# A routed expert loop: gate and up with the weights held, deeper rings, and longer lags between its stages

## The reference, cut to what matters

```python
tidx, tw = _gate(x, gate_w, gate_bias)          # 8 experts of 64, weights scaled by 2.5
w_dense = jnp.zeros((T, E), tw.dtype).at[jnp.arange(T)[:, None], tidx].add(tw)
def body(acc, ws):
    wg, wu, wdn, cw = ws                        # 256x128, 256x128, 128x256
    hmid = jax.nn.silu(x @ wg) * (x @ wu)
    return (acc + cw[:, None] * (hmid @ wdn), None)
y, _ = jax.lax.scan(body, jnp.zeros_like(x), (We_gate, We_up, We_down, w_dense.T))
```

## Time and profile before

| | us |
|---|---|
| median of 3 runs (lowest, highest) | 973.32 (966.68, 979.72) |
| the profiled execution | 971.8 |
| its span, first to last instruction | 970.0 |
| expert loop, first index copy to last scatter | 654 to 938 |

### The profile page before, as it was taken

How to read it: one execution, slowest core, us unless ns; L and a number is a source line. 1 busy time by engine, 2 the same in 40 slices (tenths; PEclk the granted TensorE clock), 3 DMA queues, 4 the chain that set the end, 5 groups by cost and what they waited for, 6 DMA issues and landing times. The chain is left out here.

```text
span 970.0 us, 19279 instructions
## 1 busy us (share of the span) xinstructions
PE 754.2 (78%) x6571; PEld 492.9 (51%) x6571; DVE 468.9 (48%) x1284; ACT 259.9 (27%) x519; POOL 269.6 (28%) x304
## 2 busy tenths in 40 slices
PE   5799998775769989989978897546768666747646
PEld 4355556454535554664457776324556445533215
DVE  4423335776745323235638868886523322322216
ACT  1121214744502121212644302231112211211150
POOL 1020002013412000000315611406556655654420
PEclk9899999998869999979985568877778877887778
DMA  9999991101887999812972101007666656658858
GB/s 342 386 354 397 412 405 57 37 2 36 317 318 271 341 411 390 348 34 48 212 172 67 39 4 43 1 1 254 199 180 214 207 183 195 210 170 254 254 182 317
DMA packets 70781, 200.40 MB, mean 207 GB/s; under 512 B 11912, under 2 KB 37744, under 8 KB 64944
## 3 DMA queue, kind: packets, MB, share of 16 engines
q1 hardware_dynamic: 60720, 176.29, 52.3%
q0 software_dynamic: 7680, 20.98, 7.0%
q10 hardware_dynamic: 2304, 2.10, 0.7%
HBM read 185.51 MB, written 13.83 MB: 206 GB/s over the span
## 5 line engine op out<-in xcount | busy, mean ns | idle before, releaser
L2000 PE MATMUL ps<-moe_wset,moe_xgT 128*128 128x256 f32 (+1 forms) x320 | 109.7, 477 | 58.4 <-issue 25.5
L2120 POOL DMA_INDIRECT moe_xg<-xn_rows,moe_idx x80 | 78.5, 981 | 111.1 <-DVE moe_idx L2069 85.8
L2000 PEld LDWEIGHTS ps<-moe_wset,moe_xgT 128*128 128x128 f32 (+1 forms) x320 | 64.9, 226 | 76.0 <-issue 56.0
L2129 POOL DMA_INDIRECT y_rows<-moe_ysb,moe_row x80 | 79.1, 989 | 42.9 <-issue 29.0
L2082 DVE TENSOR_TENSOR moe_hrow<-moe_hs,ps 128x128 f32<-128x128 f32 x80 | 22.9, 287 | 107.0 <-ACT moe_hs L2104 74.2
L2104 ACT ACTIVATE moe_hs<-ps 128x128 f32<-128x128 f32 x80 | 22.3, 278 | 163.4 <-PE ps L2000 98.4
L1469 POOL TENSOR_TENSOR ss_dec<-ss_dec,ss_cT 128x256 f32<-128x256 f32 x48 | 39.7, 862 | 91.0 <-ACT ss_dec L1424 51.1
L2077 DVE COPY moe_xgT<-ps 128x256 f32<-128x256 f32 x80 | 33.9, 424 | 62.3 <-remote 36.8
L2015 PE MATMUL ps<-moe_wset,moe_hT 128*128 128x256 f32 (+1 forms) x160 | 59.9, 463 | 3.2 <-issue 2.1
L1282 PE MATMUL ps<-xnT,w_win 128*128 128x512 f32 x128 | 58.4, 614 | 0.0
L299 PE MATMUL ps<-x0ctxT,x0qcur 128*64 128x512 f32 (+1 forms) x256 | 48.5, 534 | 7.5 <-issue 5.4
(11 more groups left out here) (404 smaller groups left out, 1424.2 us busy)
## 6 DMA issues: line engine op xcount, KB each, us to landing
x0ctxT<-ctx_T SPq DMA_DIRECT2D x8, 3202.0 KB, 18.2
x1ctxT<-ctx_T SPq DMA_DIRECT2D x8, 3202.0 KB, 13.0
x0ctxN<-ctx SPq DMA_DIRECT2D x8, 3072.0 KB
x1ctxN<-ctx SPq DMA_DIRECT2D x8, 3072.0 KB
moe_wset<-moe_gate_up SPq DMA_DIRECT2D x80, 256.0 KB
moe_wset<-L_ffn_We_down SPq DMA_DIRECT2D x80, 128.0 KB
moe_yg<-y_rows SPq DMA_DIRECT2D x7, 1024.0 KB, 10.9
ss_dec<-seg_rows SPq DMA_DIRECT2D x8, 768.0 KB, 17.0
```

What stands on the lines that cost most here:

```text
L2000: mm = pe.matmul(ps[c * n_:(c + 1) * n_, 2 + a2, 0:2 * FE], xgT[:, a2, h, c * n_:(c + 1) * n_], src[:, aw, h, :], start=h == 0, stop=h == ...
L2120: nc.gpsimd.indirect_dma_start(out=xg[:, a4, :], out_offset=None, in_=xn_rows, in_offset=bass.IndirectOffsetOnAxis(ap=idx[:, a4:a4 + 1], a ...
L2129: nc.gpsimd.indirect_dma_start(out=y_rows, out_offset=bass.IndirectOffsetOnAxis(ap=row[:, a4:a4 + 1], axis=0), in_=ysb[:, a4, :], in_offse ...
```

## The change

Gate and up: the weights become the stationary operand and the turned token rows move, so the product comes out turned (hidden units on partitions, tokens in columns), gate in PSUM columns 0 to 127 and up in 128 to 255 of the same bank. The turning of the hidden rows (`turn_hidden`), its copy `hT`, and two semaphores go. In a halves tile both experts write all 128 partitions, in different columns. `xg`, `ysb`, `idx`, `row` become rings of eight, `xgT` and silu of four, the hidden product of eight; PSUM has four banks for gate and up instead of two.

The lags: TensorE's step n holds transposes(n), gate_up(n-2), down(n-6). VectorE's holds idx(n), the xgT copy(n-7), the product(n-10), row(n-12). ScalarE's holds silu(n), ysb(n-4). GpSimd's holds gather(n), scatter(n-14). SP's `load` is untouched; it still waits for down of tile n-8. `diag` gets its memory ahead of the rings instead of after them, and the last block waits for eight scatter semaphores.

```diff
+            diag = own("diag", [P, NT // 2, 8, P])
-            xg = ring("xg", [P, 4, D])
-            xgT = ring("xgT", [P, 2, DH, P])
+            xg = ring("xg", [P, RING, D])
+            xgT = ring("xgT", [P, 4, DH, P])
-            ysb = ring("ysb", [P, 4, D])
-            hrow = ring("hrow", [P, 2, FE])
+            ysb = ring("ysb", [P, RING, D])
+            silu = ring("silu", [P, 4, FE])
+            hidT = ring("hidT", [P, RING, FE])
...
+            GU, DOWN, AHEAD = 2, 6, 7
...
                     def gate_up(n, m, g, late):
-                        wait(pe, s_hh, k - 1)
+                        wait(pe, s_hh, k - 3)
                         n_ = P if late is None else P // 2
-                        for h in range(DH):
+                        for x in range(2):
                             for c, src in enumerate((wset,) if late is None else (wset, wset2)):
-                                mm = pe.matmul(ps[c * n_:(c + 1) * n_, 2 + a2, 0:2 * FE], xgT[:, a2, h, c * n_:(c + 1) * n_],
-                                               src[:, aw, h, :], start=h == 0, stop=h == DH - 1)
+                                for h in range(DH):
+                                    mm = pe.matmul(ps[:, 2 + a4, x * P + c * n_:x * P + (c + 1) * n_], src[:, a8, h, x * FE:(x + 1) * FE],
+                                                   xgT[:, a4, h, c * n_:(c + 1) * n_], start=h == 0, stop=h == DH - 1)
                         mm.then_inc(s_gu, 1)
-                    def turn_hidden(n, m):
...
-                        pe.transpose(ps[:, 6 + a2, 0:P], hrow[:, a2, :], ident[:]).then_inc(s_hx, 1)
                     def down(n, m, g, late):
-                        k, (a4, a2) = n - 3, slots(m, 3)
-                        pe.wait_ge(s_hc, k + 1)
+                        k, a8, b = n - DOWN, (m - DOWN) % RING, (m - DOWN) % 2
+                        pe.wait_ge(s_hh, k + 1)
...
 vector:
-                        if isinstance(n, int) and n == 3:
+                        if isinstance(n, int) and n == AHEAD - 1:
                             for i in range(8):
                                 weight_third(i)
-                        if live(3):
+                        lag = AHEAD
+                        if live(lag):
...
+                        lag = AHEAD + GU + 1
+                        if live(lag):
...
+                            nc.vector.tensor_tensor(hidT[:, a8, :], silu[:, a4, :], ps[:, 2 + a4, P:2 * P], ALU.mult).then_inc(s_hh, 1)
+                        lag = AHEAD + DOWN - 1
...
 gpsimd:
-                        if live(7):
+                        lag = AHEAD + DOWN + 1
+                        if live(lag):
...
 last block, sync:
-                    for m in range(4):
-                        sp.wait_ge(s_ys[m], rounds * (RING // 4 * 16))
+                    for m in range(RING):
+                        sp.wait_ge(s_ys[m], rounds * 16)
```

More of the change, by code:

```diff
@@ L2036, in _ @@
                         transposes(first * RING + m, m, first)
-                        gate_up(first * RING + m, m, first, 0 if m >= 1 else None)
-                        turn_hidden(first * RING + m, m)
-                        down(first * RING + m, m, first, 0 if m >= 3 else None)
+                        gate_up(first * RING + m, m, first, 0 if m >= GU else None)
+                        down(first * RING + m, m, first, 0 if m >= DOWN else None)
                     with pe.Fori(1, second) as late:
@@ L2090, in step @@
                             if not early(k):
-                                dve.wait_ge(s_ys[a4], turn_of(g, m, 6) * 16)
-                            nc.vector.tensor_scalar(row[:, a4:a4 + 1], rowt[:, ds(k, 1)], 0, None, ALU.add).then_inc(s_rw, 1)
-                        if isinstance(n, int) and 4 <= n < 16:
-                            for i in ((n + 4,) if n < 12 else (2 * n - 8, 2 * n - 7)):
+                                dve.wait_ge(s_ys[a8], turn_of(g, m, lag) * 16)
+                            nc.vector.tensor_scalar(row[:, a8:a8 + 1], rowt[:, ds(k, 1)], 0, None, ALU.add).then_inc(s_rw, 1)
@@ L2095, in step @@
+                        if isinstance(n, int) and 7 <= n < 16:
+                            for i in ((n + 1,) if n < 9 else (2 * n - 8, 2 * n - 7)):
                                 weight_third(i)
-                    run(dve, step, 6)
+                    run(dve, step, AHEAD + DOWN - 1)
                 @block.scalar
@@ L2100, in step @@
                         if live(0):
-                            k, (a4, a2) = n, slots(m, 0)
+                            k, a4 = n, m % 4
                             act.wait_ge(s_gu, k + 1)
-                            wait(act, s_hh, k - 1)
-                            nc.scalar.activation(hs[:, a2, :], ps[:, 2 + a2, 0:P], ACT.Silu).then_inc(s_si, 1)
-                        if live(2):
-                            k, (a4, a2) = n - 2, slots(m, 2)
+                            wait(act, s_hh, k - 3)
+                            nc.scalar.activation(silu[:, a4, :], ps[:, 2 + a4, 0:P], ACT.Silu).then_inc(s_si, 1)
+                        lag = DOWN - GU
+                        if live(lag):
+                            k, a8, b = n - lag, (m - lag) % RING, (m - lag) % 2
                             act.wait_ge(s_dn, k + 1)
                             if not early(k):
-                                act.wait_ge(s_ys[a4], turn_of(g, m, 2) * 16)
-                            nc.scalar.copy(ysb[:, a4, :], ps[:, 4 + a2, 0:D]).then_inc(s_yc, 1)
-                    run(act, step, 2)
+                                act.wait_ge(s_ys[a8], turn_of(g, m, lag) * 16)
+                            nc.scalar.copy(ysb[:, a8, :], ps[:, 6 + b, 0:D]).then_inc(s_yc, 1)
+                    run(act, step, DOWN - GU)
                 @block.gpsimd
@@ L2128, in step @@
                             pool.wait_ge(s_rw, ready)
-                            nc.gpsimd.indirect_dma_start(out=y_rows, out_offset=bass.IndirectOffsetOnAxis(ap=row[:, a4:a4 + 1], axis=0),
-                                                         in_=ysb[:, a4, :], in_offset=None).then_inc(s_ys[a4], 16)
-                    run(pool, step, 7)
+                            nc.gpsimd.indirect_dma_start(out=y_rows, out_offset=bass.IndirectOffsetOnAxis(ap=row[:, a8:a8 + 1], axis=0),
+                                                         in_=ysb[:, a8, :], in_offset=None).then_inc(s_ys[a8], 16)
+                    run(pool, step, AHEAD + DOWN + 1)
                 @block.sync
@@ L2158, in experts @@
             s_ya = sem("moe_result_added")
-            diag = own("diag", [P, NT // 2, 8, P])
             s_dg = sem("moe_weight_diagonals")
```

91 lines of the change are left out of this document (33 added, 58 removed).

## The result

The changed kernel takes 995.6 us (median of 4 runs, 993.2 to 998.5) against 975.4 for the kernel before (4 runs, 966.7 to 979.7): ratio 1.021, 95% interval 1.016 to 1.026. It is slower by 20 us; I had forecast no change. Whether it is slower by more than 2% the interval leaves open. The profiled execution took 998.5 us, its span is 996.7.

What follows compares the result with a forecast made beforehand. SP's instruction stream was taken to set the end of the expert loop. From 971.8 us, +1 (halves tiles), +2.6 (tail) and -4 (down six behind) gave 971 us, no change; the range was 936 to 1004 us.

Steps and rivals of the forecast that it cites:

- the cover of the halves tiles: Halves tiles: 15 us more TensorE work hides behind SP's 3.8 us a tile; only +1 us exposed after the last load.
- the third rival: Halves tiles: at 1.2 GHz TensorE's 2.5 us become 5, over SP's 3.8; all 15 us exposed, 986 us; chance 0.08.
- longer runs on GpSimd: Slower rival: more tiles in flight join GpSimd's runs, slowing SP's stream, +32 us, 1004 us; chance 0.24.
- Whole-tile gate/up: Whole tiles: eight 128-column passes take 0.84 to 0.9 us against 0.86 for four of 256; value 0.
- Down six behind: Start and round trips: load 8 goes later, but SP's waits for down may shrink; +5 to -7, taken as -4 us.
- the tail: End of the loop: five downs and scatters follow the last gate/up where three did; +2.6 us.
- Gathers ahead: Gathers seven ahead, rings of eight: indirect DMAs stay 160 and transfers get slack they do not lack; value 0 on the path.
- Diag and the eight semaphores: Before the collecting loads: moved diag buffer and a wait on eight semaphores instead of four, 0 to +1 us.
- SP's mix of paces: SP's loads, fast 1.9 us or slow 4.7 us a tile: present mix stays, 0, within bounds of -45 and +92 us.
- SP's stream sets the end: Expert loop: SP's instruction stream, 3.5 us a load against TensorE's 3.2 us a tile, sets when the loop ends.
- the 80 loads in 265 to 275 us: Sign that the forecast is right: SP's 80 loads take this long from first to last issue.
- the pass step of 0.11 us: Sign that the forecast is right: sixteen gate/up passes 0.11 us apart in halves tiles.

Runs made afterwards that it cites:

- e4_held: Kernel before with only the new gate/up form (weights held in all tiles, no turn), its rings, lags and gathers kept: 991.06 us, ratio 1.011 to before.
- e1_twice: Changed kernel, but in halves tiles each expert's 64 rows go through twice in one 128-column pass: 976.98 us, ratio 1.001 to the kernel before.
- e3_deep: Changed kernel's rings, lags and gathers, but the old gate/up form and the turn in all tiles: 978.4 us, ratio 1.003 to the kernel before.
- e8_held_twice: e4_held with each half's rows sent through twice: 977.13 us, ratio 0.996 to the kernel before.
- e2_mixed: Changed kernel with the old gate/up form in halves tiles alone, turn and copy back in every tile: 978.96 us, ratio 0.999 to the kernel before.
- e5_down4: e1_twice with down four steps behind instead of six: 983.09 us, ratio 1.006 to the kernel before.
- e7_act: e1_twice with the down weights loaded by ScalarE's queue instead of SP's: 971.41 us, ratio 0.990 to the kernel before.
- e6_plain: Kernel before with each indirect scatter replaced by a plain DMA of the same bytes to consecutive rows: 891.54 us, ratio 0.906.
- e11_plain_gather: Kernel before with each indirect gather, not the scatter, replaced by a plain DMA of 128 consecutive rows: 887.36 us, ratio 0.906.

## Why the prediction was wrong

*The step that failed* is the cover of the halves tiles: "SP brings a halves tile every 3.8 us, and TensorE would need 0.22 + 1.8 + 0.43 = 2.5 us". The count of passes (sixteen) and their price at 2.4 GHz were right: 1.80 us in e4_held. But I priced TensorE at the higher clock in a stage in which it had stood at 0.78 on average, both levels by turns, and took the clock as something that the stage keeps. The new passes keep it at 1.2 GHz, a tile takes 4.9 us, and TensorE is the bound. That was the third rival: against e1_twice, the halves stage is 14.6 us longer. I gave it a chance of 0.08. That its price of 15 us fits is partly luck: 15 us is the added work at the higher clock, while the rival's own condition, 5 us a tile over SP's 3.8, gives 1.2 x 16 = 19 us. And 995.6 us lies under the 1004 of my range for another reason than the one that put 1004 there, which was longer runs on GpSimd.

*Why the clock stays down.* The rows show when it falls: after an idle time of 4.1 us in e4_held, of 6.3 us in the changed kernel. The 64-column passes do not bring it down: the first sixteen of e4_held run at the higher clock. But under them it does not rise again (73 and 67 us busy without a pause at 0.50), while the same number of passes with 128 columns each, after an idle time of 7.4 us and at the same 0.50, has it back within 6 us (e1_twice, 0.92 over the stage and no loss). The Trainium skill, "TensorE: Matmul & The Clock Gate", section "What's actually happening", says that the gate is set by how busy the engine has been. By that rule alone 73 busy us would have ended at full clock; they did not. Here the measurement decides: TensorE can be busy all the time by the trace and stay at 1.2 GHz. That the narrow passes are the cause is shown by the runs; by what way they act on the clock is not.

*Whole-tile gate/up, value 0.* Right: from gate/up 0 to 63 it is 198.2 us against 200.9, and 202.3 in e4_held.

*Down six behind, -4 within +5 to -7, and the tail +2.6.* TensorE starts 1.5 us later after the first load. Load 8 goes 19.9 us after it where it was 13.0: +6.9, not the 4.7 that I priced, and not for my reason, since load 7 is already 4.7 us late. The tail came at +3.9. Of it the lag is +1.1 to +1.8 (8.2 us in e3_deep and 8.9 in e1_twice, against 7.1 before); the rest I put down to the low clock of the last downs (e4_held against e8_held_twice, with the same lags: 8.4 and 6.3). Of the gain, gate/up 0 to 79 shows 2 to 3 us (e3_deep 267.1, e1_twice and e2_mixed 266.0, before 269.2), in single traces; e5_down4, with the shorter lag, takes 273.6. The time of e3_deep is that of before, so start, tail and gain cancel within what can be told.

*Gathers ahead, value 0 on the path.* Right as far as the runs show. GpSimd has less to do in the halves stage (19 us of 59, against 28 of 70), but e5_down4, which keeps the gathers seven ahead and only shortens down's lag, has a halves stage of 66.8 us, so the gathers ahead do not by themselves make it shorter. They have a cost at the start: load 7, with no down to wait for, is late in every kernel with seven gathers ahead whose down weights SP loads (14.5 to 18.7 us after the first load), and at 11.3 to 11.6 in every one without. What makes it late I did not test.

*Diag and the eight semaphores, 0 to +1.* From the last scatter to the end it is 34.9 us against 32.4, but the kernels that share this part with the changed one range from 32.5 to 34.9; no run shows a cost.

*SP's mix of paces, 0.* Right as a number: loads over 273.0 us, slow time 129 against 136 us. But "SP's stream sets the end" was half of it. When SP has less to issue the whole tiles take the same time (e7_act), and SP waits for TensorE, whose signals are late in the same stretches. Nor does SP's slow time by itself set the pace: it is 102 us in e4_held and 151 in e7_act, with whole tiles of 205.1 and 203.4 us. That GpSimd's indirect DMAs, which I saw only as a coincidence in the earlier trace rows, have a part in both paces is shown by e6_plain and e11_plain_gather; through what they act, and whether by number or by distance, is open.

*The test of the text.* Of its signs, the 80 loads in 265 to 275 us and the lead under 3 tiles came true, the pass step of 0.11 us did not (0.21), and the sign of the third rival did: TensorE busy right up to each load of a halves tile, and beyond.

## What to carry to other kernels

Price a TensorE-side edit at both clock levels, and let the cover hold at the lower one. In two kernels here passes of 64 columns, each behind a load of 128, kept the engine at the lower clock once it was there; try wider passes, even with columns that are thrown away, or keep that form for the wide tiles alone. When a loop is cut at landmarks, look on which side of each the long waits fall. And when a loop of small steps is slow on several engines at once and one engine issues indirect DMAs throughout, replace one kind of them by plain ones in a test kernel before counting instructions anywhere else.

## What was not expected of the hardware

- Doubling the columns of 256 passes made them faster: sixteen 64-column passes took 3.45 us (0.50), sixteen of 128 columns 1.9 us (0.92).
- Replacing either of two indirect DMAs a tile by a plain DMA of the same bytes gave 9.4%, and took SP's slow time from 136 to 13 and 14 us. GpSimd was no less occupied than before (93 of 129 us, against 125 of 209).
- An added memset of 0.33 us after each of GpSimd's 160 indirect DMAs made the kernel 1.4% faster, with SP still slow for 116 us. This is measured and not explained.
